# Expert matrices in 16 KB blocks of the arena, tokens turned two tiles ahead, piece splits and a scatter moved, adds of the last stage shared with GpSimd

## What is computed

```python
x = _layernorm(x + attention(x, wq, wk, wv, wo))
# feed-forward part, xt = x as 4096 rows:
logits = clip(xt @ gate_w.T, -50, 50)
top_w, top_idx = top_k(logits, 2)
rw = softmax(top_w)
deltas = softmax(expert_atom_weights) @ atoms          # 8 experts x 4096 entries
weighted = deltas * sigmoid(importance)
rows, cols = mask_idx // H, mask_idx % H
vals = einsum('tk,tks->ts', rw, weighted[top_idx])
contrib = segment_sum((xt[:, cols] * vals).T, rows)
out = xt @ W.T + contrib.T
x = _layernorm(x + out)
```

## Time and profile before

| | us |
|---|---|
| median of 3 runs | 1967.25 (1961.86 to 1971.83) |
| the profiled execution | 1963.19 |
| its span, the basis of all positions in the trace | 1961.4 |

### The profile page before, as it was taken

One profiled execution on the slowest core, in us unless ns is written; L12 is line 12 of the kernel. 1 busy time (PEld: TensorE's weight loads), 2 busy tenths in 40 slices (PEclk: granted clock), 3 DMA queues, 4 the chain that ended last, 5 costly groups with the idle time before them and its releaser, 6 DMA issues.

```text
span 1961.4 us, 33974 instructions
## 1 busy us (share of the span) xinstructions
PE 1838.7 (94%) x9525; PEld 1557.9 (79%) x9525; DVE 1224.3 (62%) x3794; ACT 777.4 (40%) x1985; POOL 910.3 (46%) x1274
## 2 busy tenths in 40 slices
PE   6899999999999999999999999999999986989990
PEld 6788888888888888888887888788888875778870
DVE  4445547775777577757776777677767764553444
ACT  1244434443444444444443444344434431233442
POOL 6266434433433433343334565456532334777761
PEclk6799999999999999999999999999999998999995
DMA  8543353334333433333335656565634256445777
GB/s 292 167 167 135 119 219 117 117 118 141 109 120 118 141 108 123 114 130 120 117 108 163 195 181 194 167 198 174 193 137 145 76 230 253 157 147 200 267 242 278
DMA packets 151975, 318.77 MB, mean 163 GB/s; under 512 B 18905, under 2 KB 62185, under 8 KB 140841
## 3 DMA queue, kind: packets, MB, share of 16 engines
q1 hardware_dynamic: 132320, 273.06, 41.1%
q0 software_dynamic: 19472, 43.49, 7.0%
HBM read 226.38 MB, written 90.12 MB: 161 GB/s over the span
## 4 chain that ended last, share of the span: by engine, by line
PE 73%; issue 6%; DVE 6%; POOL 5%; ACT 3%; DMA 2%; POOLq 1%; DVEq 0%; ACTq 0%; SPq 0%
PE psum L1211 19%; PE psum L1213 19%; PE psum L1212 19%; PE psum L1238 6%; PE psum L1800 3%; PE psum L1802 3%; PE psum L1801 3%; ACT probs L1438 2%; DVE pT_lo L1534 1%; PE psum L1789 1%; POOL expert_slots L442 1%; POOL expert_weights L1120 1%; POOL probs L1100 1%; DMA attn_residual<-y_acc 1%; DMA route_rows<-attn_residual 1%
## 5 line engine op out<-in xcount | busy, mean ns | idle before, releaser
L1100 POOL TENSOR_SCALAR probs<-probs,row_inv 128x128 f32<-128x128 f32 (+3 forms) x512 | 307.6, 633 | 411.5 <-DVE row_inv L1531 410.3
L1438 ACT ACTIVATE probs<-probs,neg_max 128x512 f32<-128x512 f32 (+3 forms) x512 | 282.5, 554 | 358.6 <-DVE neg_max L1523 356.5
L1211 PE MATMUL psum<-xT_hi,w_hi 128*128 128x512 f32 x640 | 253.4, 396 | 8.3 <-PEq L594 3.7
L1213 PE MATMUL psum<-xT_hi,w_lo 128*128 128x512 f32 x640 | 251.0, 392 | 0.0
L1212 PE MATMUL psum<-xT_lo,w_hi 128*128 128x512 f32 x640 | 250.5, 391 | 0.0
L1523 DVE CUSTOM_DVE_ANT_0 probs<-psum,causal 128x512 f32<-128x512 f32 (+3 forms) x512 | 223.0, 487 | 31.8 <-issue 11.7
L1534 DVE TENSOR_TENSOR pT_lo<-psum,pT_hi 128x512 fp32r<-128x512 f32 (+1 forms) x384 | 206.5, 593 | 21.2 <-ACT pT_hi L1448 21.2
L1211 PE MATMUL psum<-wo_hi,oT_hi 128*128 128x512 f32 x512 | 203.4, 397 | 4.6 <-DVE y_acc L1558 4.2
L1448 ACT CAST pT_hi<-psum 128x512 fp32r<-128x512 f32 (+1 forms) x384 | 172.5, 526 | 72.5 <-PE psum L1238 72.4
L1213 PE MATMUL psum<-wo_hi,oT_lo 128*128 128x512 f32 x512 | 200.1, 391 | 0.0
L487 DVE CUSTOM_DVE_ANT_0 route_product<-route_rows,route_gate 128x512 f32<-128x512 f32 x256 | 199.9, 797 | 0.1
(11 more groups left out here) (197 smaller groups left out, 3918.7 us busy)
## 6 DMA issues: line engine op xcount, KB each, us to landing
w_hi<-split_qk_weights SPq DMA_DIRECT2D x140, 256.0 KB, 2.7
w_lo<-split_qk_weights SPq DMA_DIRECT2D x140, 256.0 KB, 3.0
wo_hi<-split_out_weights SPq DMA_DIRECT2D x28, 1024.0 KB
wo_lo<-split_out_weights SPq DMA_DIRECT2D x28, 1024.0 KB
expert_weights_hi_lo<-split_expert_weights SPq DMA_DIRECT2D x8, 2048.0 KB, 18.2
x_in<-in_L_attn_x_dram SPq DMA_DIRECT2D x8, 1024.0 KB
expert_weights<-fill_sb SPq DMA_DIRECT2D x4, 2048.0 KB, 8.8
attn_residual<-y_acc SPq DMA_DIRECT2D x8, 1024.0 KB, 4.5
```

The lines of the kernel that those rows point to most:

```text
L1100: last = pool.tensor_scalar(p, p, row_inv[:, buf, i:i + 1], 1.0, ALU.mult, ALU.mult)
L1211: pe.matmul(dst, hi_s, hi_m, start=start, stop=False)
L1213: return pe.matmul(dst, lo_s, hi_m, start=False, stop=stop)
L1438: last = act.activation(probs[:, buf, a:a + w], probs[:, buf, a:a + w], ACT.Exp, bias=neg_max[:, buf, i:i + 1], scale=-1.0, accum_out=row_ ...
```

## The change

It has six parts. The second scatter of a group moves on GpSimd from the end of the group to right behind normalize(n + 3, 1). In the split batches both pieces are split behind that normalisation, where before one was split ahead of it; piece_raw has two buffers, and SyncE issues both loads at a group's start, ahead of route_load, and the store of the first piece behind the first weight slot. The arena is laid out so that experts 1 to 4 need not wait for the end of attention, and their loads move ahead of the fetch of wo_hi and wo_lo in the last group. In batch 7 the table steps are spread, the last group is written out anew, and `route_logits` uses one product buffer. In the expert stage tokens are turned two tiles ahead with three buffers of tokT, rstd stands ahead of the send on GpSimd, and a routed tile has five steps and not seven. In the last stage the second add of each pair is GpSimd's.

The constants, and where the tiles of the arena lie:

```diff
+AHEAD, TOKEN_BUFS = 2, 3
+BANK_RANK, BANK_TURN, BANK_ROWS = 0, 1, 4
...
+        self.piece_raw = arena("piece_raw", [P, 2, PIECE * NE])
+        self.piece_hi, self.piece_lo = arena("piece_hi", [P, NE, PIECE], F32R), arena("piece_lo", [P, NE, PIECE], F32R)
...
-        self.v_hi, self.v_lo = arena("v_hi", [P, TT, HD], F32R), arena("v_lo", [P, TT, HD], F32R)
+        self.v_lo = arena("v_lo", [P, TT, HD], F32R)
         self.probs = arena("probs", [P, 2, PACK])
         self.pT_hi, self.pT_lo = arena("pT_hi", [P, 2, PACK], F32R), arena("pT_lo", [P, 2, PACK], F32R)
-        self.piece_raw = arena("piece_raw", [P, PIECE * NE])
-        self.piece_hi, self.piece_lo = arena("piece_hi", [P, NE, PIECE], F32R), arena("piece_lo", [P, NE, PIECE], F32R)
```

SyncE: both loads of a group's pieces ahead of route_load, the store of the first behind the first weight slot, the expert matrices in another order:

```diff
-                load_piece(b, 2 * g)
+                for half in range(2):
+                    load_piece(b, 2 * g + half)
...
+            if kind == "end":
+
+                sp.wait_ge(s_seed, NB)
+                sp.wait_ge(s_xt, NB * C)
+                sp.wait_ge(s_vg, 2 * NIT)
+                load_expert(1)
+                sp.wait_ge(s_q, NIT * G)
+                load_expert(3)
+                load_expert(4)
+                sp.wait_ge(E.s_tables, 1)
+                load_expert(2)
...
-            if job == "split":
-                keep_piece(b, 2 * g)
-                load_piece(b, 2 * g + 1)
             for j in range(3):
                 slot(j, it + 2, second)
+                if job == "split" and j == 0:
+                    keep_piece(b, 2 * g)
...
-                if g == HKV - 2:
-                    sp.wait_ge(s_seed, NB)
-                    sp.wait_ge(s_xt, NB * C)
-                    sp.wait_ge(s_vg, 2 * NIT)
-                    load_expert(1)
                 if g == HKV - 1:
-                    sp.wait_ge(s_q, NIT * G)
-                    load_expert(2)
-                    load_expert(3)
                     sp.wait_ge(s_qk, 3 * NIT * G)
-                    load_expert(4)
+                    load_expert(5)
                     sp.wait_ge(s_o, NIT * G)
-                    sp.wait_ge(E.s_tables, 1)
-                    for e in range(5, NE):
-                        load_expert(e)
+                    load_expert(6)
+                    load_expert(7)
```

GpSimd: the second scatter and the splits behind normalize(n + 3, 1):

```diff
+            normalize(n + 3, 1)
+            if job == "scatter":
+                scatter((it - SCATTER_BATCHES[0] * HKV) * 2 + 1)
             if job == "split":
-                split_piece(b, 2 * g)
-            normalize(n + 3, 1)
-            if job == "split":
-                split_piece(b, 2 * g + 1)
+                for half in range(2):
+                    split_piece(b, g, 2 * g + half)
...
-            if job == "scatter":
-                scatter((it - SCATTER_BATCHES[0] * HKV) * 2 + 1)
```

TensorE in the last group of attention:

```diff
+        def last_group(it, n, route, segment):
+            out_rows(2, it - 1, "group", route)
+            scores(n + 3, 1)
+            pe.wait_ge(s_vg, 2 * it + 2)
+            pe.wait_ge(s_pt_lo, 3 * (n + 2) + 3)
+            pe.wait_ge(s_y_acc, it * TT + TT - 1)
+            values(n, 0, 0, "end")
+            pe.wait_ge(s_max, 3 * (n + 3) + 1)
+            values(n, 0, 1, "end")
+            transposes(n + 2, 0)
+            out_rows(3, it - 1, "spare", route)
+            transposes(n + 3, 1)
+            pe.wait_ge(s_max, 3 * NIT * G)
+            for j in range(AHEAD):
+                turn_tokens(pe, E, psum, ident, j)
+            pe.wait_ge(s_o_lo, n + 1)
+            values(n, 1, 0, "end", True)
+            pe.wait_ge(s_pt_lo, 3 * (n + 3) + 3 + 3)
+            values(n, 1, 1, "end")
+            out_rows(0, it, "end", route)
+            out_rows(1, it, "end", route)
+            route_ranks(pe, R, it - TT, segment, upper, ones, BANKS_PT[0])
+            out_rows(2, it, "end", route)
+            out_rows(3, it, "end", route)
```

VectorE in batch 7 (the table steps that stood together at a group's end, and their new places):

```diff
+            if job == "last":
+                if g == 1:
+                    table_sums_low(dve, E, table)
+                if g == 2:
+                    table_behind(dve, E, table)
...
+                table_numbers(dve, E, table)
...
+            if job == "last" and g == 1:
+                dve.wait_ge(s_entry, 2 * NJ)
+                table_sums_high(dve, E, table)
+                keep_ids(dve, E, 0)
+            if job == "last" and g == 2:
+                table_experts(dve, E, table)
...
-            if job == "last":
-                if g == 0:
-                    dve.wait_ge(s_entry, 2 * NJ)
-                    keep_ids(dve, E, 0)
-                    expert_ends(dve, E, table)
-                if g == 1:
-                    tiles_behind(dve, E, table)
-                if g == 2:
-                    tile_numbers(dve, E, table)
```

The expert stage, GpSimd (and the adds of the last stage), TensorE and VectorE:

```diff
+            for tt, step in routed(j):
+                if step == 1:
+                    route_rstd(pool, R, tt)
+            u, step, some = paired(j)
+            if some and step == 3:
+                rstd_of(u)
             if j:
                 send(j - 1)
-            tt, step, begun, ranked = routed(j)
-            if ranked and step == 1:
-                route_place(pool, R, tt - 1)
-                if tt == NT:
-                    pool.iota(table.tile_at_i[:], pattern=[[1, SEG_TILES]], base=0, channel_multiplier=0).then_inc(E.s_tile_at, 1)
-            if begun and step == 2:
-                route_rstd(pool, R, tt)
-            u, step, some = paired(j)
-            if some and step == 2:
-                rstd_of(u)
+            for tt, step in routed(j):
+                if step == 6:
+                    route_place(pool, R, tt)
+                    if tt == NT - 1:
+                        pool.iota(table.tile_at_i[:], pattern=[[1, SEG_TILES]], base=0, channel_multiplier=0
+                                  ).then_inc(E.s_tile_at, 1)
         send(JT - 1)
+
+        def add_second(u):
+            pool.wait_ge(s_left_in[u - PAIRS], 32)
+            y0, y1, z, _ = rows_of(u)
+            pool.tensor_tensor(z[:, 1], y0[:, 1], y1[:, 1], ALU.add).then_inc(s_used_pool, 1)
+
+        add_second(PAIRS)
         for v in range(PAIRS_LEFT):
+            if v + 1 < PAIRS_LEFT:
+                add_second(PAIRS + v + 1)
             rstd_of(PAIRS + v)
...
+            if j + AHEAD < JT:
+                pe.wait_ge(E.s_lo, j + 1)
+                turn_tokens(pe, E, psum, ident, j + AHEAD)
...
-            for t in range(2):
+            for t in range(2 if u < PAIRS else 1):
                 dve.tensor_tensor(z[:, t], y0[:, t], y1[:, t], ALU.add).then_inc(s_used, 1)
...
-                dve.wait_ge(s_used, 2 * u + t + 1)
+                if t and u >= PAIRS:
+                    dve.wait_ge(s_used_pool, u - PAIRS + 1)
+                else:
+                    dve.wait_ge(s_used, min(u, PAIRS) + u + t + 1)
```

288 lines of the change are left out of this document (161 added, 127 removed).

## The result

The changed kernel takes 1998.49 us (median of 4 runs, 1998.2 to 2001.33). The ratio to the kernel before is 1.0156, 95% interval 1.0124 to 1.0189: slower. Its profiled execution took 1998.23, its span is 1996.4, 35.0 above that of before.

A forecast was written before the change was run, and what follows sets the result against it. TensorE, nearly always busy, was taken as the bound up to the end of the expert stage. Terms summed to +6: 1963.2 (profiled execution) + 6 + 4.1 (median above it) = 1973 us, range 1934 to 1990.

The forecast's parts named there:

- (g): Expert stage: turning two tiles ahead and rstd ahead of the send remove TensorE waits and slow clock; -12.
- the change does nothing in the expert stage: Expert stage, DMA or GpSimd bound: its saving is nothing, putting 12 on any case; no chance of its own.
- (c): Split batches: later splits and stores plus an extra load delay the routed rows; six TensorE waits of 5.2, +31.
- (d): Split batches: TensorE's clock drops after each of the six waits, 1.7 each; +10, bounds 0 and 20.
- (b): Split batches: splits moved away from the two-input logit products remove two TensorE waits for oT_lo; -5.2.
- (a): Scatter batches: GpSimd's moved second scatter hides in idle time, removing twelve TensorE waits for pT_lo; -6.6.
- (f): Before the expert stage: expert matrices load earlier, so the first expert product comes sooner; -9.
- (e): Batch 7, groups 0 to 2: spread table steps take 1 of 4.0 off TensorE's output-row waits; -1.
- (h): Last stage: one add of each pair moves to GpSimd; -1, between -4.8 and +5.6.
- the loss branch: Last stage: GpSimd's add holds up VectorE's own add, some 0.7 a pair lost; +5.6.
- The +1: Last stage, by the skill's rule: both adds run one after the other, statistics beside them; +1 instead of -1.
- The main case: Split batches: six TensorE waits of 4 to 6.5 with some slow clock; 1973, 1962 to 1986, chance 0.50.

The follow-up runs named there:

- e15: The kernel before with tokens turned two tiles ahead in the expert stage, a third tokT buffer, nothing else of the change; ratio to before 1.0071.
- e14: As e13, but with tokens turned two tiles ahead, as in the changed kernel; ratio to the kernel before 0.9994.
- e13: As e11, with six tiles instead of five per routed tile, begun one earlier, rank products behind the multiplication; 1946.6 us, ratio to before 0.9914.
- e11: Changed kernel with route_load ahead of piece loads, tokens one tile ahead, rank products one tile later, GpSimd's last-stage adds beside statistics; 1959.45 us, ratio 0.9926.
- e2: Changed kernel with route_load issued ahead of both piece loads, the splits left where the change put them; ratio to the kernel before 1.0023.
- e3: Changed kernel with one piece load ahead of route_load and the second behind it, splits left in place; ratio to the kernel before 1.0108.
- e7: Changed kernel with GpSimd's last-stage second adds issued two pairs ahead and behind c_shift, beside the statistics; ratio to the kernel before 1.0132.

## Why the prediction was wrong

Forecast 1973 with 1934 to 1990, measured 1998.49. The span rose by 35 and not by 6, and 26 of the 29 us between them are one term. The 4.1 that was added for the median came out as 0.3 (1998.49 and 1998.23).

**(g), the term that failed.** Forecast -12, measured +14.1. The step was "turns tokens two tiles ahead with a third buffer: one more tile, 3.5 us, of cover". That is so for ScalarE and VectorE: of the 12.7 us 10.8 were to go, and 12.1 did. But the turn itself moved a tile earlier, and what stands ahead of it in the chain, GpSimd's fetch, did not: it is issued four tiles ahead as before. Its lead over the turn shrank by the tile that the split of the tokens gained. I had priced GpSimd's lateness at 3 as a lag of the whole engine, and didn't ask who reads the fetched rows and when. e15 (+11.1) and e14 against e13 (+12.1) show the price. The term also has nothing for the routed tile's five steps instead of seven, in which choice and ranks stand too close: e11 against e13 gives the spacing 11.3 when it isn't hidden. In the stage 12.1 us of waits went and 20.3 came, 8.2 more. The other 5.9 go with the clock, 0.95 for 0.98 in the windows of the stage, from which the term had expected 4.6 back. The rival nearest to this, "the change does nothing in the expert stage", was given 12 and no chance of its own.

**(c), right in its mechanism and size.** Forecast 31 of waits, measured 26.5 less 0.2: six waits for y_acc, 3.7 to 4.9. Its terms hold too. It starts the normalisation at 1114.9, which none of its rows shows, but against VectorE's chain of ranks the stores of the second piece were issued 3.3 to 4.4 later than before (forecast 3.3 to 3.8). From their issue to the statistics of the rows it took 9.9 to 10.5 (forecast 11). Of the 26.5, 10.1 go with the extra load and 16.2 with the late stores ahead of the load that always stood there. Hidden behind them was a third cause that I hadn't: VectorE's small instructions beside GpSimd's, most likely, which make 6.0 when the rows come first (e2).

**(d), right.** The split batches lost 34.3. TensorE's waits rose by 23.8 (from 6.0 to 29.8), and 10.5 are left, with a clock of 0.96 for 1.00. Forecast 10. e3, with waits of 2.1 to 3.3, leaves 3.6 at a clock of 0.99, and with e2's waits of 0.7 to 1.5 the clock stays at 1.00.

**(b), -5.2.** The two waits for oT_lo are gone. In their place stand eight waits of up to 0.5 for pT_lo, 3.3 in all (two before, 0.6), whose cause I didn't take apart. The two together come to -2.5.

**(a), -6.6.** Measured -6.0 to -6.1, with and without the rest of the change.

**(f) and (e), -10 together, measured -6.8.** The first expert product came 9.4 earlier after the last store. Batch 7 was 2.6 longer and not 1 shorter. All of the 4.0 for y_acc went, but TensorE waited 4.9 for token rows fetched while the DMA engines were busy to 0.96, which I had said would land in time; its waits in the batch are 12.1 in all where they were 11.9, and the other 2.4 stay open. The rows had to land before the turn, which the change had moved into the last group, not before the last matrix.

**(h), -1.** Measured +2.4, the loss branch, but it is another instruction that is held up: GpSimd's add holds up c_shift, 1.28 for 0.23. The Trainium skill, "SBUF — State Buffer", section "Who interferes with whom", names instructions with two SBUF inputs, and frees those with at most one outside the 2-port perf modes. c_shift reads two tiles in SBUF, the statistics one, and e7 agrees with the rule: beside the statistics the same add costs them nothing. The +1 that I had worked out by it took the wrong pair of instructions.

The 2.9 of batch 0 are in no term. Nearly unchanged code ran it in 267.2 to 271.1 over these executions.

The main case, 0.50, came true for the split batches; the time left the range through a term whose bounds were -20 and -5, with no loss among them. The trace of before gave reason to put one in: in the earlier trace rows GpSimd's queue holds VectorE up by 4.15, and a fetch in that queue can be as late.

## What to carry to other kernels

When a stage of a pipeline is moved one step ahead, every stage ahead of it in the chain loses that step; ask for each producer when it issues, how long it takes to land, and what can stand in its queue. Two waits in the same tile hide each other: a repair that moves a wait and gains little calls for a look at what the engine waits for next, and for the two together. A load that nobody needs soon belongs behind the one that somebody waits for in the same queue, and work of GpSimd belongs beside VectorE instructions that a trace shows undisturbed by it; here these were the statistics, with one input in SBUF.

## What the runs showed of the hardware

VectorE instructions of 128x8 and 128x1 with 0.15 to 0.4 us of work took 1.3 to 2.9 beside a GpSimd instruction, about as long as that one had left: route_chosen 2.90 beside piece_lo 3.00, a pair of c_shift 1.28 beside an add of 1.25. The statistics of 128x512 beside the same add took 0.64 each, as alone. A 512 KB load ahead of a 256 KB one in SyncE's queue, behind two stores and at a DMA share of 0.98 (1080 to 1090 us in after), went with 1.1 to 1.7 us more of TensorE's wait.
